# Gate gathers in pairs, and later counts for GpSimd's looks in an edge loop

## The chip, the cores and the metric

One core of a Trainium2 chip runs the program. The metric is the device time of one execution in microseconds (us), the median of three runs. Engines are named as the profile names them: PE is TensorE, DVE is VectorE, ACT is ScalarE, POOL is GpSimd, SP is SyncE.

## The reference

Two message-passing layers on a graph of 6250 nodes and 100000 edges, sorted by their destination, with 128 features for a node and 64 for an edge. Cut to what is computed:

```python
# layer 0
msgs = z[dst] @ Wd + z[src] @ Ws + w[:, None] * ww + bm
agg = segment_max(msgs, dst);  agg = where(deg > 0, agg, 0)
x1 = layernorm(x + relu(z @ W1a + agg @ W1b + b1) @ W2 + b2)
# layer 1, on x1
h = x1 @ node_fc_W + node_fc_b;  he = edge_features @ edge_fc_W + edge_fc_b
a = sum(h[src] * h[dst], -1)                       # a score for each edge
g = sigmoid(mlp_m(he))                             # three gates for each edge
alpha = segment_softmax(a, dst);  beta = segment_softmax(g, dst)
h_att = segment_sum(alpha * (h[src] @ node_att_W)) / 3
h_rel = segment_sum(sum_m beta_m * (h[src] @ rel_att_W_m)) / 3
h_out = where(deg > 0, relu([h_att, h_rel] @ out_fc_W + b), h)
gate = sigmoid(x1 @ gate_W + gate_b)
out = layernorm(x1 + gate * h_out + (1 - gate) * x1)
```

## The kernel before

Edges are cut into 782 tiles of 128, nodes into 49 blocks of 128. The program has five phases with a barrier of all engines between them.

1. `phase_tables` makes tables for the edge tiles and the product x @ Ws, and stores them.
2. `phase_runs` gathers the product's rows for all edges (L209), takes the running maximum, and beside it computes the gates of layer 1.
3. `phase_nodes0`, the node stage: GpSimd gathers the 49 blocks of maxima (L1009), TensorE turns them (`turn_rows`, L1026), and TensorE, VectorE and ScalarE compute x1 and h in 13 chunks of four blocks. `h_rows` (L1061) gives the rows of h of a chunk and counts them on semaphore `hp`; SP stores them. Then GpSimd gathers the gates in eight transfers of 1536 bytes a partition (L1012, `jgs`). TensorE turns them in 24 transposes (`turn_gates`, L1069): 12 after the 12th chunk's work, 8 and 4 later. Last in its queue GpSimd clears the semaphores of the phase before (L103).
4. `phase_edges`, the edge stage. In its prologue TensorE computes h once more in columns, 13 products (L1328, counted on `hcp`), and ScalarE copies them (L1400). Then the edge loop.
5. `phase_nodes1` computes the output.

**The edge loop.** A group is four tiles; there are 196 groups with those padded in. Rows of h for a tile come with one indirect DMA of GpSimd (L462), four to a group, from the table `h` in HBM into one of eight slots. A loop iteration handles eight groups. The engines are ordered by semaphores alone, and each walks its own program, in which a pass n holds work for several groups:

- TensorE, pass n: turn the rows of group n+4 (`turn_rows`, L1338, counted on `tp`), scores of n+3 (L1346, `sT`), spread of n+2 (L1355, `vv`), turned weights of n+1 (L1361, `pt`), sums of n (L1369 and L1372, `ug`).
- ScalarE: copy of the turned rows (L1411), windows of h (L1420), penalty (L1447), copy of the weights (L1452), rescale (L1438, L1440), exponentials (L1458 to L1463).
- VectorE: lowest of n+3 (L1513), picks (L1521), gate weights of n+1 (L1205, L1531), references of n+2 (L1546 to L1552), next indices once in four groups (L1578, `idxr`), and four additions of the windows of n (L1570).
- GpSimd: `gather_rows` (L454). The first eight groups are gathered without a wait beyond their indices. In the loop, for group g (slot q = g mod 8), it waits for counts of TensorE and VectorE before its 1st and its 3rd gather. `hold` (L935) is an empty instruction that keeps a wait in its place.

The semaphores of the loop start with a credit of eight, so that a wait for `NG + q - LAG + 1 + NG` on `tp` asks for that many groups plus eight. SP loads small tables for each half iteration.

## Time and profile before

| | us |
|---|---|
| median of three runs | 2734.76 |
| lowest and highest run | 2730.05, 2759.01 |
| profiled execution, its own time | 2743.96 |
| its span, first to last instruction | 2742.2 |
| `phase_edges` in it, about | 1346 to 2650 |
| the edge loop's groups from the ninth on | 1404 to 2614 |

The profile is that of one execution. A group of instructions is a line, an engine and an operation; "idle before" is the time in which the engine did nothing before them, and the names behind the arrows tell what ended it: another instruction, a DMA, "issue" (nothing that the profile shows) or "remote" (something that it does not name). Instructions of the sequencers (waits, branches, register operations) are not counted as busy.

### The profile page before, as it was taken

How to read it: one execution, taken by the hardware profiler on the slowest of the kernel's cores; microseconds unless marked ns; L12 is line 12 of the kernel's file. 1: busy time of each engine (PE TensorE's matmuls, PEld its weight loads, DVE VectorE, ACT ScalarE, POOL GpSimd, SP SyncE). 2: the span in 40 equal slices, each digit the busy share in tenths (PEclk: the TensorE clock that was granted, in tenths of full speed). 3: DMA queues.
4: the chain of work that ended last, by engine and by line, in shares of the span. 5: the costliest groups of instructions: out<-in, count | busy, mean ns of one | idle time of the engine just before them, and what ended most of it. 6: DMA issues, size and time to landing. Idle time of an engine off the chain costs nothing. (4 is left out here: it accounts for less than half of the span.)

```text
span 2742.2 us, 43228 instructions
## 1 busy us (share of the span) xinstructions
PE 1835.3 (67%) x9891; PEld 1131.7 (41%) x9891; DVE 1333.0 (49%) x5220; ACT 1117.0 (41%) x3305; POOL 1648.3 (60%) x1705
## 2 busy tenths in 40 slices
PE   3577776776767676554656776767667666666675
PEld 3222222221222222113445665656556565565565
DVE  3555555554434344324634544445445544554459
ACT  1233333333333333332444544444444444444448
POOL 3766666666767677646455655556565565655625
PEclk8798888888889798786867777777877777877788
DMA  8433333333333233322411211211222121211213
GB/s 226 167 116 125 106 118 108 118 106 123 108 105 121 87 122 108 114 87 73 129 43 48 52 50 50 53 47 54 52 50 50 52 50 52 52 49 52 54 42 114
DMA packets 115984, 235.04 MB, mean 86 GB/s; under 512 B 32910, under 2 KB 68231, under 8 KB 106423
## 3 DMA queue, kind: packets, MB, share of 16 engines
q0 software_dynamic: 52832, 109.39, 16.2%
q1 hardware_dynamic: 56522, 97.21, 9.6%
q10 hardware_dynamic: 6540, 27.42, 2.9%
q8 instruction: 36, 0.59, 0.1%
q14 instruction: 54, 0.43, 0.1%
HBM read 166.01 MB, written 67.89 MB: 85 GB/s over the span
## 5 line engine op out<-in xcount | busy, mean ns | idle before, releaser
L462 POOL DMA_INDIRECT d_region<-d_h,d_region x784 | 750.2, 957 | 549.7 <-issue 241.4
L209 POOL DMA_INDIRECT acc<-d_src_product,b_region x784 | 785.0, 1001 | 381.5 <-issue 204.6
L642 PE MATMUL banks<-acc,b_region 64*128 64x512 f32 x1176 | 340.5, 685 | 274.0 <-ACT gate_col L747 130.1
L850 DVE SCALAR_TENSOR_TENSOR acc<-b_region,acc 128x128 f32<-128x128 f32 x784 | 271.2, 346 | 364.8 <-DMA acc<-d_src_product,b_region 343.7
L1570 DVE TENSOR_TENSOR acc<-acc,banks 128x160 f32 x784 | 252.6, 322 | 346.1 <-remote 148.0
L1369 PE MATMUL banks<-d_region 128*128 128x128 f32 x1568 | 303.7, 353 | 11.6 <-issue 11.6
L642 PEld LDWEIGHTS banks<-acc,b_region 64*128 64x128 f32 x1176 | 104.9, 202 | 469.3 <-issue 180.2
L1372 PE MATMUL banks<-d_region,pick 128*128 128x128 f32 x1568 | 288.9, 341 | 11.8 <-issue 11.7
L1372 PEld LDWEIGHTS banks<-d_region,pick 128*128 128x128 f32 x1568 | 271.4, 257 | 14.7 <-issue 14.7
L1369 PEld LDWEIGHTS banks<-d_region 128*128 128x128 f32 x1568 | 268.9, 257 | 18.3 <-issue 12.8
L861 DVE SCALAR_TENSOR_TENSOR acc<-acc,b_region 128x128 f32<-128x128 f32 x784 | 270.1, 345 | 9.5 <-remote 5.7
L1355 PE MATMUL banks<-d_region 128*128 128x8 f32 x392 | 89.5, 301 | 223.9 <-DVE d_region L1552 158.3
L747 ACT ACTIVATE gate_col<-banks,b_region 128x1024 f32<-128x1024 f32 x147 | 159.3, 1112 | 163.4 <-PE banks L642 86.1
L769 ACT ACTIVATE acc<-banks 64x512 f32<-64x512 f32 x98 | 57.9, 591 | 407.8 <-remote 266.3
L747 ACT ACTIVATE acc<-banks,b_region 128x1024 f32<-128x1024 f32 x147 | 158.9, 1112 | 119.8 <-PE banks L642 64.8
L1458 ACT ACTIVATE d_region<-d_region 128x128 f32<-128x128 f32 x196 | 78.8, 402 | 283.5 <-DVE d_region L1552 177.1
L1355 PEld LDWEIGHTS banks<-d_region 128*128 128x128 f32 x392 | 75.3, 240 | 278.8 <-issue 263.7
L1338 PE MATMUL banks<-shift_ident,d_region 128*128 128x128 f32 x784 | 148.1, 321 | 36.4 <-ACT d_region L1411 24.5
L1346 PE MATMUL banks<-d_region 128*32 128x128 f32 x1568 | 95.6, 320 | 108.5 <-DVE d_region L1513 82.1
L654 PE MATMUL banks<-acc,b_region 128*32 128x512 f32 x588 | 163.7, 700 | 0.0
L1411 ACT ACTIVATE d_region<-banks 128x512 f32<-128x512 f32 x196 | 114.8, 586 | 119.8 <-remote 103.4
L654 PE MATMUL banks<-gate_col,b_region 128*32 128x512 f32 x588 | 156.8, 674 | 0.8 <-ACT acc L769 0.8
(261 smaller groups left out, 2439.0 us busy)
## 6 DMA issues: line engine op xcount, KB each, us to landing
d_runs<-acc SPq DMA_DIRECT2D x48, 1024.0 KB
acc<-ea ACTq DMA_DIRECT2D x25, 1024.0 KB
acc<-d_src_product,b_region POOLq DMA_INDIRECT x784
d_region<-d_h,d_region POOLq DMA_INDIRECT x784
d_region<-d_rel SPq DMA_DIRECT2D x49, 256.0 KB
hT<-xT SPq DMA_DIRECT2D x7, 448.0 KB, 7.0
d_src_product<-acc SPq DMA_DIRECT2D x7, 448.0 KB, 3.1
d_gates<-acc ACTq DMA_DIRECT2D x196, 6.0 KB
```

The source lines that it names most:

```text
L209: pool.indirect_dma_start(self.rows[:, s, j, :], None, d["B"], bass.IndirectOffsetOnAxis(self.idx[:, k:k + 1], 0)).then_inc(self.gathered[ ...
L462: pool.indirect_dma_start(rows[:, s, :], None, table, bass.IndirectOffsetOnAxis(idx[:, s:s + 1], 0)).then_inc(gathered[q], 16)
L642: last = nc.tensor.matmul(bank[4 + n % 2 * 2 + h][:, :], wf[h * DE:(h + 1) * DE, m * P:(m + 1) * P], ea[h * DE:(h + 1) * DE, u % (2 * UC), ...
L654: last = nc.tensor.matmul(bank[3][h * W:(h + 1) * W, :], w2m[:, m * W:(m + 1) * W], rt[u % 2][m][:, h * G4:(h + 1) * G4], start=(m == 0), ...
L747: nc.scalar.activation(rt[u % 2][m].rearrange("p (h e) -> p h e", h=2), two(4 + n % 2 * 2, 0, G4), ACT.Relu, bias=bf[:, m:m + 1]).then_inc ...
L850: nc.vector.scalar_tensor_tensor(rows[:, s, j, :], wwb, wgt[:, k:k + 1], rows[:, s, j, :], ALU.mult, ALU.add).then_inc(ch, 1)
L861: nc.vector.scalar_tensor_tensor(H[:, k % n, :], H[:, (k - 1) % n, :], rst[:, k:k + 1], rows[:, s, j, :], ALU.add, ALU.max).then_inc(ch, 1)
L1338: last = nc.tensor.transpose(TURNED[:, j * P:(j + 1) * P], rows[:, s * GJ + j, :], ident[:, :])
L1355: nc.tensor.matmul(BOUNDS[:, 0:8], vals[q % 2][:, 8:9].to_broadcast([P, P]), sel[q % 2][:, 0:8], start=True, stop=True).then_inc(vv, 1)
L1369: nc.tensor.matmul(U[q % 2][:, :, j, :], rows[:, s * GJ + j, :], wts[q % 2][:, j, :, :], start=True, stop=True)
L1372: last = nc.tensor.matmul(Z[q % 2], pick[:, M - k:M - k + P], wts[q % 2][:, :, k, :], start=(k == 0), stop=(k == M))
L1570: nc.vector.tensor_tensor(w, w, UZ[q % 2][:, :, j, :], ALU.add).then_inc(ad, 1)
```

## The change

It adds no computation and moves no data to another place.

- **Gate gathers.** Before the 1st, 3rd, 5th and 7th of the eight, GpSimd waits until `h_rows` has counted 10, 11, 12 and 13 chunks. TensorE's 24 transposes all move behind its other work of the stage.
- **First eight groups of the edge stage.** GpSimd waits for 4, 8 and 13 column products before groups 2, 3 and 4, and for the first, second and third turning before groups 5, 6 and 7.
- **Edge loop.** The wait before the 1st gather of a group keeps indices and space. The counts of TensorE are asked for before the 2nd gather (spread and turned weights) and before the 4th (turned rows and scores), and are later ones.

```diff
@@ gather_rows
     for q in range(NG):
+        if q in PRODUCTS_BY:
+            pool.wait_ge(products_done, PRODUCTS_BY[q])
+        if q in TURNED_BY:
+            pool.wait_ge(rows_turned, TURNED_BY[q] + NG)
         gathers(q)
...
         for q in range(NG):
-            pool.wait_ge(rows_turned, it * NG + (NG + q - LAG + 1 + NG))
             pool.wait_ge(idx_ready, it * NG + (NG + q + 1))
             pool.wait_ge(rows_used, it * NG + (NG + q + 1))
-            gathers(q, range(0, GJ // 2))
-            pool.wait_ge(weights_turned, it * NG + (NG + q - LAGW + 1 + NG))
-            gathers(q, range(GJ // 2, GJ))
+            gathers(q, range(0, 1))
+            pool.wait_ge(spread, it * NG + (NG + q - 3 + NG))
+            pool.wait_ge(weights_turned, it * NG + (NG + q - 4 + NG))
+            gathers(q, range(1, 3))
+            pool.wait_ge(rows_turned, it * NG + (NG + q + NG))
+            pool.wait_ge(scored, it * NG + (NG + q - 1 + NG))
+            gathers(q, range(3, GJ))
...
+PRODUCTS_BY = {2: 4, 3: 8, 4: 13}
+TURNED_BY = {5: 1, 6: 2, 7: 3}
@@ phase_nodes0, GpSimd
             for k in range(JC):
+                if k % 2 == 0:
+                    pool.wait_ge(hp, NC4 - JC // 2 + 1 + k // 2)
                 pool.indirect_dma_start(jg[:, k, :, :].rearrange("p m e -> p (m e)"), None, d["gates"][0:TC * P, :],
@@ phase_nodes0, TensorE
-                if n == NC4 - 2:
-                    pe.wait_ge(jgs, 16 * JC)
-                    pe.wait_ge(mx, NC4)
-                    turn_gates(0, 1, 2)
-                if n == NC4 - 1:
-                    pe.wait_ge(va, NC4)
-                    turn_gates(3, 7)
+            pe.wait_ge(jgs, 16 * JC)
+            pe.wait_ge(mx, NC4)
+            pe.wait_ge(va, NC4)
             pe.wait_ge(xtc, NC4)
-            turn_gates(4)
+            turn_gates(*GATE_BANKS)
```

## Rows read from the trace of the kernel before

**Rows 1.** Stage table, edge loop: busy us (count) PE, PEld, DVE, ACT, POOL; clock.

```profile
1404.00:2614.00 1210.00, 834.84 (x5798) 717.60 (x5797) 594.91 (x2665) 566.11 (x2430) 716.12 (x748) 0.77 0.20 51
```

**Rows 2.** Lines, edge loop: busy us, mean ns | idle before, releasers.

```profile
L462 POOL DMA_INDIRECT d_region<-d_h,d_region x748 | 716.1, 957 | 508.6 <-issue 200.3 <-remote 157.0 <-PE banks L1372 57.5
...
L1570 DVE TENSOR_TENSOR acc<-acc,banks 128x160 f32 x749 | 241.3, 322 | 335.4 <-remote 145.3 <-issue 90.3 <-PE banks L1372 15.9
...
L1411 ACT ACTIVATE d_region<-banks 128x512 f32<-128x512 f32 x187 | 109.5, 585 | 103.1 <-remote 93.7 <-PE banks L1338 5.3 <-PE banks L1346 2.7
...
L1346 PE MATMUL banks<-d_region 128*32 128x128 f32 x1496 | 90.6, 318 | 107.6 <-DVE d_region L1513 81.3 <-issue 26.1
...
L1355 PE MATMUL banks<-d_region 128*128 128x8 f32 x374 | 85.4, 301 | 219.9 <-DVE d_region L1552 154.3 <-issue 65.2
...
L1513 DVE CUSTOM_DVE_ANT_0 d_region<-d_region,banks 128x128 f32<-128x128 f32 x187 | 54.3, 290 | 108.7 <-issue 51.1 <-remote 43.3 <-PE banks L1355 2.0
```

**Rows 3.** Timeline, edge loop: start, us, engine, line [idle before <-releaser].

```profile
2009.58 0.95 POOL L462 DMA_INDIRECT d_region<-d_h,d_region  x1 [0.45 <-issue]
...
2013.90 0.95 POOL L462 DMA_INDIRECT d_region<-d_h,d_region  x1 [2.00 <-PE banks L1338]
...
2046.12 0.95 POOL L462 DMA_INDIRECT d_region<-d_h,d_region  x1 [2.11 <-PE banks L1372]
...
2054.87 0.95 POOL L462 DMA_INDIRECT d_region<-d_h,d_region  x1 [0.30 <-issue]
...
2058.53 1.12 POOL L462 DMA_INDIRECT d_region<-d_h,d_region  x1 [2.71 <-remote]
...
2056.90 0.29 DVE L1513 CUSTOM_DVE_ANT_0 d_region<-d_region,banks 128x128 f32<-128x128 f32 x1 [1.92 <-issue]
...
2055.11 0.29 ACT L1438 ACTIVATE acc<-acc,d_region  x1 [3.31 <-issue]
...
2057.34 0.42 PE L1346 MATMUL banks<-d_region 128*32 128x128 f32 x8 [2.69 <-issue]
```

**Rows 4.** Timeline of the node stage, and line L103 (ns min/median/max).

```profile
1317.44 0.94 POOL L1012 DMA_INDIRECT acc<-d_gates,tile_of_job  x1 [0.30 <-issue]
...
1320.89 1.09 PE L1052 MATMUL banks<-shift_ident,n_region 128*128 128x128 f32 x4 [9.98 <-issue]
...
1336.92 1.47 PE L1069 MATMUL banks<-shift_ident,acc 128*128 128x128 f32 x12
...
1342.94 0.46 PE L1061 MATMUL banks<-n_region,hT 128*128 128x129 f32 x2 [0.94 <-DVE n_region L1182]
...
1343.23 0.60 PE L1069 MATMUL banks<-shift_ident,acc 128*128 128x128 f32 x4
...
L103 POOLq EVENT_SEMAPHORE_RANGE_CLEAR  x78: 3/44/708, 1205.1 to 2619.1; - x78
```

**Rows 5.** Timeline of ScalarE in the prologue of the edge stage.

```profile
1368.60 0.69 ACT L1400 ACTIVATE hT<-banks,d_region 128x512 f32<-128x512 f32 x1 [3.52 <-remote]
...
1392.38 0.60 ACT L1411 ACTIVATE d_region<-banks 128x512 f32<-128x512 f32 x1 [8.03 <-remote]
```

**Rows 6.** Timeline of TensorE in the edge loop.

```profile
2012.07 1.06 PE L1338 MATMUL banks<-shift_ident,d_region 128*128 128x128 f32 x4
...
2042.30 0.43 PE L1346 MATMUL banks<-d_region 128*32 128x128 f32 x8
...
2042.90 0.30 PE L1361 MATMUL banks<-shift_ident,d_region 128*128 128x128 f32 x1
...
2047.66 0.43 PE L1346 MATMUL banks<-d_region 128*32 128x128 f32 x8 [0.98 <-DVE d_region L1513]
...
2049.87 0.45 PE L1361 MATMUL banks<-shift_ident,d_region 128*128 128x128 f32 x1
```

**Rows 7.** Timeline of the first row gathers of the node stage.

```profile
1243.01 0.95 POOL L1009 DMA_INDIRECT acc<-d_runs,end_idx  x1 [0.30 <-issue]
...
1245.62 1.08 PE L1026 MATMUL banks<-shift_ident,acc 128*128 128x128 f32 x4 [18.84 <-DMA acc<-d_runs,end_idx]
```

More of the change, by code:

```diff
@@ L451, in iterations_but_one, with gather_rows @@
     return eng.value_load(t["nit"][0:1, 1:2], min_val=MINIT - 1, max_val=MAXIT - 1)
-def gather_rows(nc, pool, t, table, idx, rows, idx_ready, rows_used, rows_turned, weights_turned, gathered, after_first):
+def gather_rows(nc, pool, t, table, idx, rows, idx_ready, rows_used, rows_turned, weights_turned, gathered, after_first,
+                products_done, scored, spread):
     rest = iterations_but_one(pool, t)
@@ L1275, in credit @@
                     nc.gpsimd.memset(start[:, n:n + 1], 0.0).then_inc(s, per * CREDIT)
-            gather_rows(nc, pool, t, d["h"], idx, rows, idxr, ug, tp, pt, gat, credit)
+            gather_rows(nc, pool, t, d["h"], idx, rows, idxr, ug, tp, pt, gat, credit, hcp, sT, vv)
             new_sems.clear_ended()
```

## Prediction

> **What bounds the kernel now.** The table of stages comes first [rows 1]: the edge loop, from 1404 to 2614 us, is 1210 of the 2742 us. It issues 748 gathers, four to a group, so it walks 187 groups at 6.47 us each. No engine is full in it: TensorE 835 us, GpSimd 716, VectorE 595, ScalarE 566.
>
> Next the list of lines in that stretch [rows 2]. A gather (L462) takes 0.957 us, and where nothing holds it the next starts 0.30 us later: four make 3.83 + 1.20 = 5.03 us, less than the period. The rest of its idle time (508.6 us, 2.72 a group, of which 1.20 are those 0.30) is longer pauses, put down to "remote" or TensorE. Who waits for the gathers? TensorE's L1355 and L1346 wait for VectorE, not for a DMA. So rows come early, and GpSimd is held by counts that lie ahead of need. But VectorE waits for no engine either: before L1570 and L1513 it idles 335.4 and 108.7 us, of which "remote" and "issue" end 145.3 + 90.3 and 43.3 + 51.1, together 330 us or 1.76 a group. ScalarE shows the same at L1411 (93.7).
>
> When do the engines stand? The timeline tells [rows 3]. From 2046.12 to 2054.87 GpSimd issues eight gathers without a break. At its end VectorE's next instruction comes 1.92 us late, ScalarE's 3.31 and TensorE's 2.69. Then GpSimd itself pauses 2.71 us. After six gathers (before 2046.12) it paused 2.11, after four (before 2013.90) 2.00. Two other stages say it louder. In the node stage the eight gate gathers follow the row gathers without a break; the last starts at 1317.44, and TensorE stands 9.98 us, until 1320.89 [rows 4]. In the prologue of the edge stage 32 gathers go out in a row, and ScalarE stands 3.52 and 8.03 us [rows 5]. So my reading: **long unbroken runs of gathers hold up the other engines' instructions**, and the run itself ends in a pause. How a gather does this no row tells. The loop is a cycle of TensorE, VectorE and ScalarE made slower by this; the cure is worth up to 1.76 us a group.
>
> **The edge loop's looks.** Let g be the group being gathered. Before, its first two gathers wait until TensorE has turned g-3, the last two until it has turned the weights of g-6; both counts fall in TensorE's pass g-7. After, the first gather waits for indices and space alone (counts of pass g-8, long there); the 2nd for the spread of g-4 and the weights of g-5, both in pass g-6; the 4th for the rows of g-1 and the scores of g-2, both in pass g-5. No work is added, only waits and register operations in GpSimd's queue. Behind a held look stands all of that queue: the rest of g and the first gather of g+1. TensorE's turning of g waits for them.
>
> In a pass TensorE gives scores at one point and turned weights later: scores at 2042.30 with L1361 at 2042.90, scores at 2047.66 with L1361 at 2049.87 [rows 6]. So the 4th gather of a group goes with the 1st of the next, and the 2nd with the 3rd: runs of two if both looks hold, of four if only the score look does. What does a held look cost? TensorE had turned a group by 2013.13 and the gather came at 2013.90: 0.77 us [rows 3, 6]. A look inside a group, at 2009.58, cost 0.45 [rows 3]. The worst end is the pause after four gathers, 2.00.
> - Both looks at 0.77: 3.83 + 2 x 0.30 + 2 x 0.77 = 5.97 us a group. I take this.
> - Both at 0.45: 3.83 + 0.60 + 0.90 = 5.33 us.
> - Runs of four, each with 2.00: 3.83 + 0.90 + 2.00 = 6.73 us.
>
> I take the first, since scores and weights are apart in one of the two passes and the pass between them (scores 2042.30 to scores 2047.66) took 5.36 us: the other engines can follow 5.97. Sum: (6.47 - 5.97) x 187 = 94 us less; bounds 213 less and 49 more.
>
> **The prologue's looks.** Groups 2, 3 and 4 wait for 4, 8 and 13 column products, groups 5 to 7 for the first three turnings, so the run of 32 breaks up. Of ScalarE's stands, 3.52 hits the products and 8.03 the first copies [rows 5]; the later gathers start later, but their rows are needed only after the products. Bounds 0 and 11.5 less; I take 5, above the first stand and under the second, since VectorE's clearing of the accumulators stays in the way.
>
> **The gate gathers.** In pairs, each pair after one more block of h rows, the last after all 13. Of the stand, TensorE's 9.98 us should go, so the last h rows end at 1333.4 and not at 1343.4. Then 0.77, two gathers (1.25), landing, and all 24 transposes, of which 20 lay between other work before. Landing is read in the first blocks: 4th gather issued at 1243.01, turned from 1245.62, so 2.61 us [rows 7]. Twelve transposes took 1.47 us, 24 then 2.9 [rows 4]; four took 1.08 in the first blocks, 24 then 6.5 [rows 7]. So 1333.4 + 0.77 + 1.25 + 2.61 + 2.9 = 1340.9, at worst 1344.5, where the last transposes ended at 1343.83 [rows 4]. SP's last stores go out 10 us earlier and are hidden. The semaphore clears that GpSimd makes behind the last gather move too, 37 of the 78, median 44 ns, up to 708 [rows 4]: 1.6 us, beside the transposes; all at the longest, 26 us, would be 18 us more on the path. Gain 0 to 3, I take 3; if the stand stays, this part costs 7 to 10.
>
> **Sum.** 94 + 5 + 3 = 102 us less. The profiled execution took 2743.96 us; the median of the three runs is 2734.76, 9.2 less. 2743.96 - 102 - 9.2 = 2633 us.
>
> **A rule that speaks against it.** The loop gathers later than before. The cycle landing (2.61), turning (1.06), ScalarE's copy (0.585), scores (0.43) and 0.77 [rows 2, 6, 7] is 5.46 us, under 5.97 but not by much. The Trainium skill (DMA: Bandwidth & Descriptors, section Rules for kernel authors) says to issue a DMA early and to wait on its semaphore late, so that its fixed cost overlaps. By that rule this part of the change gives cover away for nothing, and the sum would be that of rival 3.
>
> **Rivals.**
> 1. *Runs of four.* The weights are turned within the 0.77 us in which the 4th gather gets going, so the look at the 2nd never holds. For it: 2042.30 to 2042.90. Against: 2047.66 to 2049.87 [rows 6]. Between today's 6.47 and 6.73 us a group, 0 to 49 more, less 8 of the other parts: 2727 to 2776. Chance 0.20, two thirds of it within 1%.
> 2. *Each look pays the long pause.* Two runs of two, each with 2.00: 3.83 + 0.60 + 4.00 = 8.43, 367 more, less 8: 3094. It decides if a pause is due to waiting as such, from 1.0 us a look upward. Against: the 0.77 and 0.45. Chance 0.06.
> 3. *TensorE waits for rows (the other side).* With the score look every delay of one engine goes round the cycle of 5.46 us; one instruction late by 1.92 us [rows 3] in each makes 7.38, 170 more, less 8: 2897. From 1.0 us of such delay a group upward the kernel is slower. Chance 0.08.
> 4. *The looks change nothing.* The counts are always there and runs are as long, or the stands come from something else: 6.47, and 8 us less from the rest: 2727. Chance 0.11, a quarter of it beyond 1% through the prologue.
>
> My forecast has 0.55; its own range is 2535 (both looks near 0.45) to 2700. Range over all: 2535 to 2785, which leaves out rivals 2 and 3 and a tail below, 0.2. About 1%, 27 us, is what a measurement of this kernel tells from no change. Faster 0.58, within 1% 0.21, slower 0.21.
>
> **What would show it.** Right: no run above four gathers in the loop, mostly two; 0.4 to 0.8 us before L462 at the 2nd and 4th gather; "remote" and "issue" before L1570 and L1513 well under half; the loop about 94 us shorter; no stand of ScalarE above 3 us in node stage and prologue. Wrong: pauses of 2 us after runs of two (rival 2); L1338 waiting for DMA (rival 3); runs of four with 2 us pauses (rival 1). If runs are short and VectorE stands all the same, my reading of the cause is wrong.

## The result, and the profile after

The changed kernel takes 2729.69 us, the median of 19 runs; beside it the kernel before takes 2743.06 (19 runs). The ratio is 0.9955, its 95% interval 0.9939 to 0.9970: 12 us less, where 2633 us were forecast. It is a gain, but one of the size that the prediction called no change. The profiled execution took 2724.75 us, its span is 2723.0.

Two words are used throughout. A "look" is a wait of GpSimd for counts ahead of a gather; it is "held" when the gather had to wait. A "stand" is a stretch in which an engine does nothing and no row names what it waits for.

The table of stages of the changed kernel, with the stages cut at the same gathers as before (first gather of the node stage, first of the edge stage, the 37th, the last). Columns: window, length, busy us (count) of PE, PEld, DVE, ACT, POOL, granted clock, DMA share, GB/s.

```profile
1230.40:1341.40 111.00, 63.45 (x344) 50.57 (x344) 53.12 (x186) 39.02 (x90) 53.92 (x57) 0.75 0.35 104
1341.40:1407.10 65.70, 36.14 (x195) 21.66 (x195) 31.44 (x72) 33.80 (x102) 34.87 (x52) 0.71 0.22 57
1407.10:2600.10 1193.00, 823.01 (x5730) 690.90 (x5729) 583.88 (x2641) 574.63 (x2406) 709.91 (x748) 0.79 0.20 51
```

Cut in the same way, the kernel before had 108.1, 64.3 and 1206.4 us in these three. So the loop gave 13 us, 6.39 us a group instead of 6.46; node stage and prologue took 4 more. What lies ahead of the node stage, which the change doesn't touch, was 9 us shorter in this execution (1230.5 us for 1239.2). That is why the two profiled executions differ by more than the medians.

The lines of the loop after the change, which answer to [rows 2]. Line numbers are 8 higher, that of the gathers (L462) 1:

```profile
L463 POOL DMA_INDIRECT d_region<-d_h,d_region x747 | 709.9, 950 | 483.1 <-issue 288.9 <-remote 77.9 <-PE banks L1380 73.9
L1346 PE MATMUL banks<-shift_ident,d_region 128*128 128x128 f32 x740 | 144.0, 326 | 338.7 <-DMA d_region<-d_h,d_region 328.9 <-issue 9.8
L1363 PE MATMUL banks<-d_region 128*128 128x8 f32 x370 | 86.6, 307 | 4.3 <-issue 3.1 <-DVE d_region L1560 1.2
L1578 DVE TENSOR_TENSOR acc<-acc,banks 128x160 f32 x741 | 238.7, 322 | 308.3 <-remote 131.3 <-issue 67.2 <-PE banks L1380 20.4
L1521 DVE CUSTOM_DVE_ANT_0 d_region<-d_region,banks 128x128 f32<-128x128 f32 x186 | 54.0, 290 | 214.9 <-remote 140.1 <-PE banks L1363 52.1 <-PE banks L1354 9.0
```

Read the second line first. TensorE's turning of gathered rows now waits 328.9 us for a DMA. The same line before the change waited for no rows:

```profile
L1338 PE MATMUL banks<-shift_ident,d_region 128*128 128x128 f32 x749 | 140.2, 319 | 11.5 <-ACT d_region L1411 6.5 <-issue 4.8
```

So GpSimd is no longer far ahead, and its gathers set the pace. TensorE's waits further down the pass went in exchange: before the spread (L1363, before L1355) it stands idle for 4.3 us where it was 219.9 [rows 2]. The first line holds all of GpSimd's time in the loop, 709.9 us busy and 483.1 idle. Of the idle time 747 x 0.30 = 224 us are the shortest distance from one gather to the next; the other 259 us are pauses. Where are they? The timeline of GpSimd, and below it that of TensorE's turning (L1346), scores (L1354) and turned weights (L1369) in the same stretch:

```profile
2007.20 0.95 POOL L463 DMA_INDIRECT d_region<-d_h,d_region  x1 [1.85 <-PE banks L1380]
2008.45 0.94 POOL L463 DMA_INDIRECT d_region<-d_h,d_region  x1 [0.30 <-issue]
...
2010.95 0.95 POOL L463 DMA_INDIRECT d_region<-d_h,d_region  x1 [0.30 <-issue]
2013.58 0.95 POOL L463 DMA_INDIRECT d_region<-d_h,d_region  x1 [1.68 <-PE banks L1354]
...
2017.33 0.95 POOL L463 DMA_INDIRECT d_region<-d_h,d_region  x1 [0.30 <-issue]
2020.09 0.94 POOL L463 DMA_INDIRECT d_region<-d_h,d_region  x1 [1.82 <-PE banks L1380]
...
2009.95 1.11 PE L1346 MATMUL banks<-shift_ident,d_region 128*128 128x128 f32 x4 [3.44 <-DMA d_region<-d_h,d_region]
2016.30 0.65 PE L1346 MATMUL banks<-shift_ident,d_region 128*128 128x128 f32 x4 [0.61 <-DMA d_region<-d_h,d_region]
2016.88 0.43 PE L1354 MATMUL banks<-d_region 128*32 128x128 f32 x8
2017.48 0.31 PE L1369 MATMUL banks<-shift_ident,d_region 128*128 128x128 f32 x1
```

Runs of four: the 4th gather of a group with the first three of the next, then a pause of 1.68 to 1.85 us. 3.80 + 3 x 0.30 + 1.7 = 6.4 us is the group. The look at the 2nd gather (spread, weights) is not held: at 162 of 178 such places the gap is the usual 0.30. The look at the 4th is followed by a pause of 1.6 us or more at 137 of 178 places; the mean over all is 1.58. And the pause is not the wait for a count. The scores' count was there at 2017.31, before the run's last gather had even begun to run (2017.33 to 2018.28); the next gather still starts at 2020.09. Of the 178 looks (groups 15 to 192; a count is taken at the end of the matmuls that give it), 92 had their count within 0.2 us ahead of the start of the gather in front, and the median pause there was 1.74 us. In 11 the count came over 0.5 us ahead, and there was no pause. In none did it come after the gather in front had ended.

Did the shorter runs free the other engines? VectorE's register operations tell it without the question of what a gap is due to: they wait for nothing, and their median is 40 ns. One line of them before the change and the same after (ns min/median/max):

```profile
L1568 DVEq ALU_OP  x558: 4/40/772, 1414.1 to 2614.6; - x186
```

```profile
L1576 DVEq ALU_OP  x555: 5/40/796, 1409.5 to 2598.7; - x185
```

In both a few take some 0.7 us. Counted over the traces: of VectorE's and ScalarE's register operations and branches in the loop (about 4800), 261 took over 0.5 us before, and 34 after. So 87% of the long ones went, and 1% of the loop.

### The profile page after: what moved, and what is told of

It is laid out like the page before. It is cut to its first block and busy times, and to the rows that moved or that the text cites. A ratio compares the mean times of both kernels' runs of the same rounds, so it can differ in the third digit from the quotient of the medians.

```text
span 2723.0 us, 43327 instructions
## 1 busy us (share of the span) xinstructions
PE 1828.4 (67%) x9891; PEld 1116.2 (41%) x9891; DVE 1327.8 (49%) x5220; ACT 1130.5 (42%) x3305; POOL 1636.7 (60%) x1705
## 5 line engine op out<-in xcount | busy, mean ns | idle before, releaser
L652 PE MATMUL banks<-acc,b_region 64*128 64x512 f32 x1176 | 346.5, 696 | 260.1 <-ACT gate_col L757 128.3
L1346 PE MATMUL banks<-shift_ident,d_region 128*128 128x128 f32 x784 | 153.4, 327 | 352.1 <-DMA d_region<-d_h,d_region 328.9
L1377 PEld LDWEIGHTS banks<-d_region 128*128 128x128 f32 x1568 | 282.2, 266 | 23.9 <-issue 22.8
L1380 PE MATMUL banks<-d_region,pick 128*128 128x128 f32 x1568 | 278.1, 335 | 5.6 <-issue 3.8
L1380 PEld LDWEIGHTS banks<-d_region,pick 128*128 128x128 f32 x1568 | 264.8, 253 | 7.0 <-issue 6.9
L1346 PEld LDWEIGHTS banks<-shift_ident,d_region 128*128 128x128 f32 x784 | 100.6, 163 | 391.9 <-issue 386.7
L1521 DVE CUSTOM_DVE_ANT_0 d_region<-d_region,banks 128x128 f32<-128x128 f32 x196 | 56.8, 290 | 240.0 <-remote 162.5
L664 PE MATMUL banks<-acc,b_region 128*32 128x512 f32 x588 | 151.6, 655 | 0.0
L1539 DVE TENSOR_TENSOR d_region<-d_region,gate_col 128x384 f32<-128x384 f32 x196 | 110.0, 561 | 25.2 <-issue 1.5
```

The source lines that it names most:

```text
L652: last = nc.tensor.matmul(bank[4 + n % 2 * 2 + h][:, :], wf[h * DE:(h + 1) * DE, m * P:(m + 1) * P], ea[h * DE:(h + 1) * DE, u % (2 * UC), ...
L664: last = nc.tensor.matmul(bank[3][h * W:(h + 1) * W, :], w2m[:, m * W:(m + 1) * W], rt[u % 2][m][:, h * G4:(h + 1) * G4], start=(m == 0), ...
L1346: last = nc.tensor.transpose(TURNED[:, j * P:(j + 1) * P], rows[:, s * GJ + j, :], ident[:, :])
L1377: nc.tensor.matmul(U[q % 2][:, :, j, :], rows[:, s * GJ + j, :], wts[q % 2][:, j, :, :], start=True, stop=True)
L1380: last = nc.tensor.matmul(Z[q % 2], pick[:, M - k:M - k + P], wts[q % 2][:, :, k, :], start=(k == 0), stop=(k == M))
```

## The experiments

Unless told otherwise each kernel is the one before with the edit shown, ratios are to the kernel before on the same chip, with 95% intervals. "Long" is a register operation of VectorE or ScalarE in the loop of over 0.5 us (before: 261, after: 34). A loop is counted from the 37th to the last gather, a group is that over 186.75 (747 steps from gather to gather, over four). The letters of theories are those of the expectations.

### Each part alone

**e1_ends** holds the gate gathers and the prologue's looks, with the old loop; **e2_loop** the new looks of the loop, with the old gates and prologue.

> The kernel before with the two small parts of the change alone: gate gathers held to the counts of h rows, the 24 transposes at the end, and the looks in the first eight groups. The edge loop keeps its old looks. Theory A (the loop brought the whole gain, these parts cost): from first row gather of the node stage to first gather of the edge stage 111 us where before had 108.1, from there to the 37th gather 65.7 where it had 64.3, loop unchanged: 4 to 6 us more, ratio 1.002. Theory C (these parts brought the 12 us that the change brought, and the loop nothing): ratio 0.996.

> The kernel before with the new looks of the edge loop alone. Theory A: the loop from the 37th to the last gather takes 1193 us where before had 1206, 13 to 18 us less, ratio 0.993 to 0.995. Theory C (the ends brought the gain): ratio 1.000, loop 1206 us.

Measured: e1_ends 0.9993 (0.9975 to 1.0010), loop 1206.2 us, 279 long; e2_loop 0.9966 (0.9946 to 0.9986), loop 1196.3 us, 27 long. The loop's looks carry the gain, 10 us of it in the trace. The small parts come out at zero within the interval: the node stage takes 107.7 and 111.0 us in the two traces that have the edit (e1_ends and the changed kernel), 108.1 to 109.8 in the ten traces of the same kind of chip that don't. Theory C falls. The loop's 10 us are less than the 13 to 18 of theory A, and that the small parts cost 4 to 6 us isn't shown: the interval of e1_ends runs from 7 us less to 3 more.

### Where the look stands against its count

**e3_noscore**: the look at the 4th gather asks for the turned rows alone, whose count comes about 0.45 us sooner. **e4_late**: it asks in addition for the weights turned in the same pass, about 0.5 us later. Both on top of e2_loop.

```
@@ e3_noscore
             pool.wait_ge(rows_turned, it * NG + (NG + q + NG))
-            pool.wait_ge(scored, it * NG + (NG + q - 1 + NG))
@@ e4_late
             pool.wait_ge(scored, it * NG + (NG + q - 1 + NG))
+            pool.wait_ge(weights_turned, it * NG + (NG + q - 3 + NG))
```

> The loop's part of the change, but the 4th gather asks for the turned rows of g-1 alone, not for the scores of g-2. TensorE gives that count 0.4 to 0.7 us earlier. Theory A (a look costs GpSimd a fixed pause of about 1.7 us when its count is not there some 0.4 us before the gather in front of it starts, and nothing when it is): pauses before the 4th gather are still either 0.30 or 1.6 to 1.9 us, but fewer than 120 of 180 are long instead of 160; runs get longer; the loop lies within 30 us of the 1193 us of the changed kernel, since stands of the other engines come back with the long runs. Theory B (GpSimd follows the count at a fixed distance, 2.8 us, and the loop is the cycle landing, turning, scores, look): the cycle gets shorter by the 0.45 us between the two counts in every group, 84 us less than the changed kernel, the pause keeps its length.

> The loop's part of the change, and the 4th gather asks for the turned weights of g-4 as well, a count that TensorE gives in the same pass 0.4 to 0.8 us after the scores. Theory A: the pause is GpSimd's own as long as the count comes before the gather in front has ended by about 1 us; pauses before the 4th gather stay at 1.6 to 1.9 us, hardly any of 0.30 is left, at most 20 us more than the changed kernel. Theory B: every group gets longer by the delay of the count, 0.5 us x 187 = 94 us more.

Measured: e3_noscore 0.9955 (0.9936 to 0.9975), loop 1185.3 us; e4_late 1.0092 (1.0060 to 1.0124), loop 1225.1 us. The line of the gathers in each loop:

```profile
L463 POOL DMA_INDIRECT d_region<-d_h,d_region x747 | 709.2, 949 | 476.0 <-issue 195.3 <-remote 171.7 <-PE banks L1343 78.5
```

```profile
L463 POOL DMA_INDIRECT d_region<-d_h,d_region x748 | 706.9, 945 | 519.5 <-issue 183.2 <-PE banks L1368 159.5 <-PE banks L1379 101.5
```

A count half a microsecond later cost 29 us against e2_loop (32 against the changed kernel), not 94: the gap before the 4th gather went from 1.62 to 1.84 us in the mean, where a fixed distance from the count (theory B) would have made it longer by the whole delay. Nor did a count half a microsecond sooner bring the 84 us of theory B; it brought 11. What changed is how many looks are followed by a pause. In e3_noscore 94 of 178 4th gathers go without one, in e4_late 7; and the runs get longer, mostly six in e3_noscore:

```profile
2002.45 0.94 POOL L463 DMA_INDIRECT d_region<-d_h,d_region  x1 [2.07 <-remote]
...
2008.70 0.94 POOL L463 DMA_INDIRECT d_region<-d_h,d_region  x1 [0.30 <-issue]
2011.73 0.94 POOL L463 DMA_INDIRECT d_region<-d_h,d_region  x1 [2.09 <-remote]
```

with it the long operations: 217 in e3_noscore, 6 in e4_late. This is the trade in one pair of runs. Short runs free the others and cost GpSimd a pause each; long runs save pauses and bring the stands back. Theory B falls. Theory A is the nearer one but not exact: e4_late lost 32 us where 20 were allowed, and e3_noscore's pauses, 2.06 us in the mean, lie above its 1.6 to 1.9. Nor is every pause free of waiting there: in 33 looks of e3_noscore and 56 of e4_late the count came over 1.0 us after the start of the gather in front, so it was late indeed. Whether the third wait of e4_late has a price of its own is open.

### How fast the others are without gathers, and the loop without looks

**e5_half** issues two of a group's four gathers, so its output is not the layers'; it is there for its time alone. **e6_nolooks** drops both counts of TensorE.

```
@@ e5_half
-            gathers(q, range(0, GJ // 2))
+            gathers(q, range(0, 1))
...
-            gathers(q, range(GJ // 2, GJ))
+            gathers(q, range(1, 2))
...
-                pe.wait_ge(gat[s], it * 64 + 64 * lap(q))
+                pe.wait_ge(gat[s], it * 32 + 32 * lap(q) + 32)
@@ e6_nolooks
-            pool.wait_ge(rows_turned, it * NG + (NG + q - LAG + 1 + NG))
...
-            pool.wait_ge(weights_turned, it * NG + (NG + q - LAGW + 1 + NG))
```

> The kernel before, but from the ninth group on only the first two of a group's four gathers are issued, so the rows of the other two tiles are those of an earlier group: half of the gathers are left out, all other work stays. It measures how fast the other engines walk when gathers are no bound. Theory A (gathers in long runs cost the other engines time, and GpSimd's 6.4 us a group is the bound after the change): 5.0 to 5.6 us a group, the loop 940 to 1050 us instead of 1206. Theory D (the other engines have their 6.4 us a group from their own chain and gathers cost them nothing): the loop stays within 20 us of 1206.

> The kernel before without the two counts of TensorE ahead of a group's 1st and 3rd gather: a gather waits for its indices and for space alone (the sums of g-8). Theory A: GpSimd runs ahead until all slots are full and is then held once in a group by the count of sums: runs of four, each ended by a pause of 1.6 us or more, and so 6.4 to 6.5 us a group, the loop 1195 to 1220 us. Theory E (without the early looks runs get longer than six and the stands of the other engines grow): loop above 1230 us.

Measured: e5_half 0.868 (0.861 to 0.875), loop 845.8 us, 4.53 a group, 15 long; e6_nolooks 0.9988 (0.9964 to 1.0013), loop 1205.8 us, 188 long. The loop of e5_half in the table of stages:

```profile
1413.30:2259.00 845.70, 678.74 (x5765) 577.29 (x5764) 584.01 (x2650) 546.59 (x2417) 352.32 (x373) 0.93 0.17 44
```

and two of its lines:

```profile
L462 POOL DMA_INDIRECT d_region<-d_h,d_region x373 | 352.3, 945 | 494.7 <-PE banks L1338 251.1 <-PE banks L1361 173.8 <-issue 66.4
...
L1338 PE MATMUL banks<-shift_ident,d_region 128*128 128x128 f32 x744 | 119.6, 286 | 0.0
```

With gathers halved all other work of a group goes through in 4.53 us, less than the 5.0 to 5.6 of theory A. TensorE's own speed is part of it: it was idle for 167 us of this loop, where it was for 375 before, the clock granted to it was 0.93 instead of 0.77 [rows 1], and its busy time fell from 835 to 679 us. So the other engines have no 6.4 us of their own (theory D falls), and the floor of the loop is GpSimd's four gathers, 5.0 us. Without looks (e6_nolooks) the loop is what it was with the old ones, within 1 us, and theory E falls. GpSimd, now held by indices and space alone, makes 79 runs of four and 44 of eight, where theory A had only fours. The gap before the 1st gather is 1.68 us in the mean of 178; 51 of them are the usual 0.30, the others 2.2 in the mean, so pauses are no shorter than those behind a look of TensorE's counts.

### Breaks in the run without a held look

If only the run's length mattered, a break made by other work would do. **e7_space1** puts 15 tiny writes of GpSimd behind the 2nd gather of a group, **e8_space2** the same behind the 2nd and the 4th.

```
+            def space(n=1):
+                for k in range(15):
+                    last = nc.gpsimd.memset(start[:, k:k + 1], 0.0)
+                last.then_inc(spd, n)
...
             gathers(q, range(0, GJ // 2))
+            pool.wait_ge(spaced, it * NG + (q + NG))
+            hold(pool)
+            space()
```

> The kernel before with its looks, and between the 2nd and the 3rd gather of each group 15 small writes of GpSimd (memset, 128x1), which in the prologue took 0.55 us and lengthened the gap between two gathers from 0.30 to 0.70 us. GpSimd works 0.4 us more a group, 75 us in all, but it breaks each run of gathers without a held look. Theory F (what frees the other engines is any break in a run of gathers): their stands get shorter, the loop is 20 to 80 us shorter than 1206. Theory G (only GpSimd's pause of 1.6 us and more after a held look frees them, or the sum of GpSimd's time is what counts): the loop is as long as before or up to 75 us longer.

> As the kernel with one block of 15 small writes a group, but with two, behind the 2nd and behind the 4th gather: GpSimd works 0.8 us more a group, 150 us in all, 5.8 us a group without pauses. Theory F: no run of gathers is longer than two, the stands of the other engines are gone but for the pauses, the loop 40 to 100 us shorter than 1206. Theory G: 0 to 150 us longer.

Measured: e7_space1 0.9938 (0.9915 to 0.9961), loop 1194.4 us; e8_space2 1.0082 (1.0056 to 1.0109), loop 1230.7 us. Of e8_space2, GpSimd's timeline:

```profile
2000.65 0.95 POOL L462 DMA_INDIRECT d_region<-d_h,d_region  x1 [0.30 <-issue]
2001.60 0.51 POOL L1289 MEMSET d_region<- 128x1 f32 x15
2002.51 0.95 POOL L462 DMA_INDIRECT d_region<-d_h,d_region  x1 [0.40 <-issue]
```

the lines of the writes and of TensorE's turning in the loop:

```profile
L1289 POOL MEMSET d_region<- 128x1 f32 x5490 | 188.4, 115 | 0.4
L1353 PE MATMUL banks<-shift_ident,d_region 128*128 128x128 f32 x747 | 152.7, 339 | 394.6 <-DMA d_region<-d_h,d_region 394.6
```

and the register operations of VectorE's additions:

```profile
L1583 DVEq ALU_OP  x558: 40/40/40, 1407.0 to 2631.2; - x186
```

This is the strongest evidence that the gathers' sequence causes the stands: the edit touches GpSimd alone. With runs of two all through the loop but its last groups, not one of VectorE's 558 operations of that line takes more than 40 ns, and there is no long one on either engine. It is not the mean rate of gathers either: e4_late spreads the same gathers over 1225 us and has 6 long operations, the kernel before over 1206 us and has 261. Yet the loop of e8_space2 is slower, because GpSimd takes 6.6 us a group, and TensorE waits for rows 394.6 us. Theory F is right about the others and wrong about the time, which lies in the bounds of theory G. e7_space1 breaks the run once in four gathers by a gap of 0.97 us. It has 243 long operations, 183 of them ScalarE's, though its longest runs are four gathers, as in the changed kernel with its 34. There a pause of some 1.7 us lies between the runs, here often the 0.97. Its loop is 12 us shorter, less than the 20 of theory F. Its ratio is the lowest of all kernels that issue every gather, but the interval overlaps that of the changed kernel (0.9939 to 0.9970), so it can't be called a better version.

**e9_even1** and **e10_even3** put one and three such writes behind every gather.

```
                                     bass.IndirectOffsetOnAxis(idx[:, s:s + 1], 0)).then_inc(gathered[q], 16)
+            if spread_out:
+                space(j)
```

> The kernel before with its looks, and behind each gather of the loop one small write of GpSimd (memset, 128x1). Block of 15 such writes at one place lengthened the gap between two gathers from 0.30 to 0.97 us; one at each place should add 0.05 to 0.25 us to every gather, 5.2 to 6.0 us a group, with no gather right behind another. Theory F2 (what disturbs the other engines is how densely gathers follow each other: at 1.25 us from one to the next they stand, at 1.6 they don't): stands are fewer, pauses before the 1st gather fewer, loop 20 to 90 us shorter than 1206. Theory G (a run is a run until GpSimd really pauses for 1.6 us or more): stands and pauses as before, loop 1206 or up to 40 us longer.

> As the kernel with one small write behind each gather of the loop, with three. The distance of two gathers is 0.1 to 0.35 us above 1.25, 5.4 to 6.4 us a group. Theory F2: almost no stands, looks rarely held, GpSimd's own time is the bound, and the loop is 187 times that: 1010 to 1200 us. Theory G: loop 1206 to 1260 us.

Measured: 0.9953 (0.9933 to 0.9972) and 0.9988 (0.9970 to 1.0006), loops 1197.5 and 1199.6 us, 183 and 150 long. They don't answer their question. One write fits into the 0.30 us gap and three make it 0.32 to 0.35, so the distance of gathers hardly moved; and the count that orders the writes, asked for right after it was made, put a gap of at least 1.0 us before nearly every 1st gather of a group.

### The same kernels on chips without stands

**e11_even9** and **e12_even13** put nine and thirteen writes behind each gather, ordered by a count two groups old.

```
+            def space(j, q=0):
+                at = 8 + (q % 2 * GJ + j) * 15
+                for k in range(at, at + 9):
+                    last = nc.gpsimd.memset(t["iota_r"][:, k:k + 1], 0.0)
```

> The kernel before with its looks, and nine small writes of GpSimd (memset, 128x1) behind each gather of the loop, on cells that nothing else uses there; the count that orders them is now two groups old, so that it is never waited for. Three such writes had made the gap 0.32 to 0.35 us, each further one adds 0.028: the gap is 0.50, one gather follows the other after 1.44 us and a group takes GpSimd 5.8 us without pauses. Theory F2 (the other engines are held up by how densely gathers follow each other): fewer stands, loop 20 to 110 us shorter than 1206. Theory G (only pauses of 1.6 us and more free them): loop 1190 to 1230 us with as many stands of VectorE as before.

> As the kernel with nine small writes behind each gather, with thirteen: the gap is 0.61, the distance of two gathers 1.56 us, a group takes GpSimd 6.2 us without pauses. Theory F2: hardly a stand, looks rarely held, GpSimd's own 6.2 to 6.4 us are the period, loop 1165 to 1200 us. Theory G: 1200 to 1260 us.

They ran on a chip on which the kernel before took 2277.0 us (7 runs, 2275.7 to 2291.4), 17% less than the 2740 of all runs so far. Their ratios there are 1.0836 (1.0794 to 1.0877) and 1.1939 (1.1896 to 1.1982), so their question stayed open as well. So the two kernels of this study were run unchanged beside them, and it was again such a chip: before 2277.45 us (13 runs).

> The kernel before, unchanged, for its trace on this chip. Where the kernel before takes about 2740 us: the trace of before again, loop 1206 us within 5. Where it takes about 2277 us: 32 or more gathers in a row with 0.30 between them, no stand of ScalarE or VectorE above 1.5 us that no engine explains, 5.0 to 5.2 us a group, so GpSimd's four gathers without pauses are the bound (theory A's floor); or, if the stands were no cost (theory D), runs of six and 5.0 to 5.2 us a group from the chain of the other engines.

> The changed kernel, unchanged. Where before takes about 2740 us: 0.9955 as known. Where before takes about 2277 us: theory A (the held look costs GpSimd a pause, whether or not there are stands to be cured): runs of four and a pause, 5.6 to 6.4 us a group instead of 5.0 to 5.1, 100 to 250 us more than before, ratio 1.04 to 1.11. Theory H (the pause too belongs to the chips that show stands): pauses of 0.5 us, ratio 0.98 to 1.03.

> The kernel with nine small writes behind each gather, run again. Where before takes about 2740 us: theory F2 (density holds the others up) 1150 to 1190 us for the loop, ratio 0.98 to 0.995; theory G: 1.000 to 1.02. Where it takes about 2277 us: 1.08 as before.

> The kernel with thirteen small writes behind each gather, run again. GpSimd's time here was 7.43 us a group, more than reckoned, for a pause at the end of each iteration of the loop. Where before takes about 2740 us: GpSimd is the bound, 7.2 to 7.6 us a group, ratio 1.06 to 1.09, and no stands. Where it takes about 2277 us: 1.19 as before.

Measured: e13_before 0.9999 (0.9983 to 1.0015); **e14_after 1.0082 (1.0053 to 1.0111)**, about 20 us slower; e15_even9 1.0851 and e16_even13 1.1942, as the first time. The kernel before there, its node stage, prologue and loop:

```profile
1079.50:1164.50 85.00, 54.29 (x344) 42.88 (x344) 53.25 (x186) 39.63 (x90) 53.83 (x57) 0.86 0.47 136
1164.50:1210.00 45.50, 33.10 (x178) 19.28 (x178) 30.48 (x68) 32.02 (x92) 34.71 (x52) 0.79 0.32 81
1210.00:2160.00 950.00, 727.65 (x5810) 618.68 (x5810) 590.75 (x2673) 571.31 (x2443) 722.31 (x748) 0.86 0.26 65
```

the gathers' line in the loop:

```profile
L462 POOL DMA_INDIRECT d_region<-d_h,d_region x748 | 723.3, 967 | 227.9 <-issue 196.2 <-PE banks L1372 17.7 <-PE banks L1338 11.0
```

and VectorE's register operations:

```profile
L1568 DVEq ALU_OP  x564: 40/40/40, 1210.6 to 2157.3; - x188
```

All 748 gathers follow each other with gaps of 0.30 or 0.31 us, 5.09 us a group, and there is no pause and no long operation: GpSimd is full, the floor of theory A. The same program needs 256 us more in the loop alone where there are stands. So long runs by themselves do not bring the stands; long runs on one kind of chip do. The changed kernel on this chip, the same three stages:

```profile
1082.20:1176.40 94.20, 57.11 (x344) 45.39 (x344) 53.21 (x186) 39.69 (x90) 53.88 (x58) 0.82 0.42 123
1176.40:1224.70 48.30, 37.37 (x195) 23.14 (x195) 32.26 (x76) 34.36 (x104) 34.80 (x53) 0.75 0.30 77
1224.70:2179.00 954.30, 714.50 (x5783) 605.65 (x5783) 588.79 (x2659) 569.54 (x2423) 718.98 (x747) 0.88 0.26 64
```

Its timeline of GpSimd at two looks:

```profile
1264.93 0.94 POOL L463 DMA_INDIRECT d_region<-d_h,d_region  x1 [0.76 <-PE banks L1354]
1268.67 0.94 POOL L463 DMA_INDIRECT d_region<-d_h,d_region  x1 [0.30 <-PE banks L1354]
```

Its loop takes 954 us: the same looks, with the count again within 0.2 us ahead of the start of the gather in front in 130 of 178, and a gap of 0.30 us in each of them, where the first chip paused 1.74. Where the count came over 0.6 us after the start of the gather in front (ten looks), the next gather followed the count by 0.77 or 0.78 us. So theory A's general form fell and theory H holds: **the pause behind a look belongs to the stands; it is a stand of GpSimd itself.** The traces of the two chips show it at the wait instruction. On this one a wait that ended at 1707.45 is followed by its gather at 1707.47. On the first one GpSimd's wait ended at 2019.40, 2.1 us behind the count and 1.6 behind the register operation ahead of it, and the gather came 0.69 us later still.

**e17_space2x8** and **e18_space2x3**, two blocks of eight and of three writes, were to look for a spacing that wins where there are stands.

> As the kernel with two blocks of 15 small writes a group, with two blocks of eight. Each write less takes 0.028 us: gaps of about 0.92 and 0.74 us, 3.8 + 0.6 + 1.66 = 6.06 us a group for GpSimd. Where before takes about 2740 us: theory F2: no stands, looks not held, 6.1 us a group, loop 1135 to 1150 us, ratio 0.975; if stands come back with the shorter gaps: some looks are held, 6.3 to 6.5 us a group, loop 1175 to 1210, ratio 0.99 to 1.00. Where before takes about 2277 us: GpSimd is the bound, 6.1 us a group, ratio 1.08.

> The same with two blocks of three: gaps of about 0.78 and 0.60 us, 5.8 us a group for GpSimd. Where before takes about 2740 us: theory F2 with a limit below 5.8: loop 1085 to 1110 us, ratio 0.96; with stands back: 6.3 to 6.5 us a group, loop 1175 to 1210, ratio 0.99 to 1.00. Where before takes about 2277 us: 5.8 us a group, ratio 1.06.

They too ran on a chip without stands (before 2278.21 us): 1.0247 (1.0221 to 1.0273) and 1.0032 (1.0020 to 1.0044) where 1.08 and 1.06 were expected, loops 1000.1 and 952.8 us. A block of eight makes the gap 0.46 us there and one of three 0.32, not 0.74 to 0.92 and 0.60 to 0.78 as reckoned from e8_space2. Whether such a spacing wins on a chip with stands stays open. So does theory F2, that the distance from gather to gather counts and not the length of a run: of the kernels that space gathers by over 0.05 us, only e7_space1 and e8_space2 ran on a chip with stands, and both shorten the runs too.

## Why the prediction was wrong

The step that failed is the price of a held look: 0.77 us was put into the sum, and the mean gap was 1.58, so that a group took 6.39 us and not 5.97. The other wrong term, that both looks hold, would by itself have made the loop shorter than forecast: runs of four at 0.77 are 3.83 + 0.90 + 0.77 = 5.50 us a group.

- **What bounds the kernel.** "Rows come early, and GpSimd is held by counts that lie ahead of need": the first half is right; the second took pauses for waits. In the kernel before, groups 15 to 192 have 125 pauses of over 1.0 us before a 1st or 3rd gather, 282 us in all. In 93 of them, 206 us, the last count asked for was there before the gather in front had ended. Only 27, 66 us, ended 0.74 to 0.80 us after a late count, 20 of these being VectorE's next indices. Where nothing stands, the same kernel never pauses and the loop is GpSimd's 5.09 us a group (e13_before). That "no engine is full" was true and misleading: 5.03 us and 1.44 of pauses are the 6.47.
- **Long runs hold up the others.** Right on the chips with stands: 261 long register operations with runs of four, six and eight, 34 with runs mostly of four, none with runs of two (e8_space2); whether by their length or by how closely gathers follow is open. On the other chips it is not so at all (e13_before). The sign that I named for it, "remote" and "issue" before the additions and the lowest well under half, failed all the same: 339 us after against 330. It was a poor sign, since an engine that is not the bound idles anyhow.
- **Both looks hold, runs of two.** This step, which chose the case, failed too. The weights are turned within 0.6 us of the scores (2016.88, 2017.48), so the look at the 2nd gather found its count at 162 of 178 places. It is rival 1, given 0.20. My counter-row (2047.66 to 2049.87 [rows 6]) was no exception in the kernel before: from the scores' end to the turned weights' end a pass took 2.04 us in the median there, because TensorE waited between them for VectorE's L1552 (the 219.9 us before L1355 [rows 2]). In the changed kernel it is 0.48 us. TensorE now waits for rows ahead of its turning, VectorE is done by the time the scores are, and the wait between scores and weights is gone (4.3 us before L1363). I took a distance between two counts from the old trace and did not ask whether the change itself would alter it.
- **The price of a held look, 0.77.** 0.77 us is right for a count that comes late while GpSimd waits for it, and e14_after shows exactly that number. But behind a run of four the gap was 1.58 us in the mean (e2_loop 1.62, e4_late 1.84). The row that I priced from, 2013.90 [rows 3], is one of the 27 where the count was late: TensorE gave it at 2013.13, 1.23 us after the gather in front had ended, and 1.23 + 0.77 are the 2.00. The 0.45 at 2009.58 is the same price, 0.75 us after its count of 2008.83, part of it behind the gather in front. The next pause in the same timeline is of the common kind: its count was there at 2016.70, and the gather comes 3.76 us later.

```profile
2020.46 0.95 POOL L462 DMA_INDIRECT d_region<-d_h,d_region  x1 [1.79 <-PE banks L1372]
```

  With rival 1 and 1.58 for its 2.00 the sum is 3.80 + 0.90 + 1.58 + 0.11 = 6.39, the measured group; the 0.11 are the few looks held at the 2nd gather.
- **The other engines can follow 5.97.** Right; with half the gathers they follow 4.53 (e5_half), and 5.09 and 5.11 with all of them on a chip without stands.
- **Rival 3**, TensorE waiting for rows, named the wait (328.9 us) but not its weight. It waits because GpSimd is slow, and a delay does not go round the cycle in full: a count half a microsecond sooner or later in every group moved the loop by 11 and 29 us, not by 84 and 94 (e3_noscore, e4_late). The Trainium skill (DMA: Bandwidth & Descriptors, section Rules for kernel authors) speaks for an early issue and a late wait. By that rule the sum would have been this rival's 2897 us, and 2729.69 were measured. The lead that the rule protects did go: on the chip without stands the loop took 4.6 us more (954.4 for 949.8) and the node stage 9.2.
- **Prologue, 5 us less.** It gave 1.3 with the old loop (e1_ends 63.0 for 64.3) and 2.0 with the new one (65.7 for e2_loop's 67.7). Only two of the six looks held, and twice 12 gathers in a row remain. The stand of 8.03 became one of 7.15. GpSimd at the two held looks:

```profile
1365.06 0.94 POOL L463 DMA_INDIRECT d_region<-d_h,d_region  x1 [3.54 <-remote]
1380.83 0.94 POOL L463 DMA_INDIRECT d_region<-d_h,d_region  x1 [1.08 <-issue]
```

and ScalarE:

```profile
1379.81 0.60 ACT L1419 ACTIVATE d_region<-banks 128x512 f32<-128x512 f32 x1 [7.15 <-remote]
```

- **Gate gathers, 3 us less.** Half right. TensorE's stand of 9.98 [rows 4] went, and the last h rows ended 7.8 us sooner, 96.4 us after the first row gather where it was 104.2. But the tail behind them grew from 0.4 to 12.8 us where I had 7.5. After the change:

```profile
1320.80 0.94 POOL L1024 DMA_INDIRECT acc<-d_gates,tile_of_job  x1 [20.28 <-PE banks L1073]
...
1326.39 0.46 PE L1073 MATMUL banks<-n_region,hT 128*128 128x129 f32 x2 [0.96 <-issue]
...
1329.89 0.94 POOL L1024 DMA_INDIRECT acc<-d_gates,tile_of_job  x1 [0.30 <-issue]
1334.27 5.38 PE L1081 MATMUL banks<-shift_ident,acc 128*128 128x128 f32 x24 [7.42 <-DMA acc<-d_gates,tile_of_job]
```

and in the table of stages TensorE's stand and the transposes:

```profile
1326.90:1334.20 7.30, 0.00 (x0) 0.00 (x0) 0.36 (x2) 0.00 (x0) 3.02 (x4) 0.66 0.69 203
1334.20:1339.70 5.50, 5.38 (x24) 4.98 (x24) 0.00 (x0) 0.00 (x0) 0.00 (x0) 0.52 0.00 0
```

  Three terms. The counts for the four pairs came within 6.3 us (1320.52 to 1326.85) and eight gathers take 10.0, so the queue was behind and the last one started 3.04 us after the last h rows, not 2.0. From its issue to the first transpose it was 4.38 us, not 2.61: I had taken the landing from rows of 512 bytes [rows 7], and these have 1536; that the size is the reason isn't shown. And the 24 transposes took 5.38 us, not 2.9: TensorE had done nothing for 7.42 us and its granted clock was 0.52, the 1.2 GHz level, where those of [rows 4] ran at full clock. The Trainium skill (TensorE: Matmul & The Clock Gate, section What's actually happening) says that the array's clock is halved when it has been idle; the trace agrees. On a chip without stands, where there is nothing to cure, the h rows end only 0.6 us sooner and the same edit costs 9.2 us: 94.2 for 85.0.

In one sentence: that gathers in long runs hold up the other engines was right for these chips and the breaks do free them, but GpSimd, which had to make the breaks, was the engine next to its limit, and it paid for each with a pause of its own. Why one kind of chip has stands and the other has none, and how a gather brings them about, stays open.

## What to carry to other kernels

Before pricing a wait that is to break up an engine's run, ask what that engine needs for the run itself, and take the price from the pauses that followed runs of that length, sorted by whether their count was late or had long been there; one row can be of the rarer kind. The distance between two counts is part of the schedule that the change alters, so ask what fills it. A count asked for "just in time" is not free because it comes in time: in the changed kernel, where there were stands, only those over 0.5 us ahead of the start of the gather in front never brought a pause (11 of 11), and in e3_noscore 6 of 58 such did. And where the gain of an edit is to be the end of a stand that no row explains, time both kernels on more than one chip first: here the edit gave 0.45% with stands and took 0.8% on a chip without.

## What the runs showed of the hardware

- **The same program took 2740 us on some chips and 2277 on others.** Of the six chips of the experiments, three (e1 to e4, e5 to e8, e9 and e10) were of the first kind and three (e11 and e12, e13 to e16, e17 and e18) of the second; the 19 runs beside the result were of the first. On one chip the runs of a kernel agree within 1.2%. The granted clock of the kernel before was 0.80 to 0.82 in the runs of the first kind and 0.87 to 0.89 in those of the second, and TensorE was busy for 835 and 728 us of the loop; VectorE's and ScalarE's instructions took the same (258 and 254 ns, 296 and 296 ns in the mean), and so did the gathers (957 and 967 ns). I found nothing in the traces that names the reason: the packets of the gathers took 0.22 us in the median on both, and there are as many packets of instructions (54 and 53).
- **Where there are stands, some instructions of the sequencers that wait for nothing take about 0.7 us instead of 40 ns**, on VectorE, ScalarE and SyncE, and more of them the longer GpSimd's run of gathers: in the kernel before 0.7 in a run of four, 2.4 in one of six, 5.4 in one of eight, of the three engines together (register operations and branches of over 0.5 us). They seldom fall together: 27 of VectorE's 142 overlap one of ScalarE's. On GpSimd it shows as a pause of 1.4 to 3.0 us at the next wait.
- **A much longer loop body fetched instructions anew and paused at each turn.** With 13 more instructions behind each of 32 gathers (e12_even13) GpSimd paused some 3.3 us once an iteration, at its turn, and the page of its profile counts 189 packets of instructions in queue q14 instead of 53 (e13_before); with nine (e11_even9) it is 166. That the fetches make the pause is likely but not shown. GpSimd's timeline and the line of the page:

```profile
1689.69 0.94 POOL L462 DMA_INDIRECT d_region<-d_h,d_region  x1 [3.38 <-issue]
1750.36 0.94 POOL L462 DMA_INDIRECT d_region<-d_h,d_region  x1 [3.25 <-issue]
```

```profile
q14 instruction: 189, 1.55, 0.2%
```
